# Key products one step ahead in the plain attention steps, and four weight products of layer 3 on a PSUM bank each

## What is computed

```python
def attention(h, ctx, mask, bias, ln_w, w_q, w_k, w_v, w_out):   # layer 1: 32 heads of 128
    q = rmsnorm(h, ln_w) @ w_q.T
    k, v = ctx @ w_k.T, ctx @ w_v.T
    p = softmax(where(mask, q @ k.T + bias, -inf))
    return h + (p @ v) @ w_out.T

def lora(h):                       # layer 2: W_base, 4 active experts of rank 8, a router
    alpha = softmax(log(prior[active] + 1e-12) + (h @ router_W.T + router_b)[active])
    return h @ W_base.T + b_base + sum_e(alpha_e * (h @ A_e.T) @ B_e.T) * 2.0

def cross(h, ctx):                 # layer 3: one head, width 512
    Q, K = h @ Wq.T + bq, ctx @ Wk.T + bk
    return softmax(Q @ K.T / sqrt(512)) @ ctx

def quantised(h):                  # layer 4: 6-bit codes unpacked, scale and zero point
    return h @ dequantise(qweight).T + bias

x = x + attention(layernorm(x), ctx, ...)
x = x + lora(layernorm(x))
x = x + cross(layernorm(x), ctx)
x = x + quantised(layernorm(x))
```

## Time and profile before

| | |
|---|---|
| median of 3 runs | 986.61 us (985.14 to 986.87) |
| profiled execution | 985.75 us |
| its span, first to last instruction | 983.9 us |
| mean granted TensorE clock | 0.994 of full |
| PE busy | 954.6 us, 97% of the span |
| DVE, POOL, ACT busy | 61%, 48%, 40% |
| DMA moved | 169.60 MB, 172 GB/s |

### The profile page before, as it was taken

One profiled execution on the slowest core, in us unless ns is written; L12 is line 12 of the kernel. 1 busy time (PEld: TensorE's weight loads), 2 busy tenths in 40 slices (PEclk: granted clock), 3 DMA queues, 4 the chain that ended last, 5 costly groups with the idle time before them and its releaser, 6 DMA issues.

```text
span 983.9 us, 16715 instructions
## 1 busy us (share of the span) xinstructions
PE 954.6 (97%) x5645; PEld 835.4 (85%) x5645; DVE 603.1 (61%) x1123; ACT 395.0 (40%) x1101; POOL 470.3 (48%) x528
## 2 busy tenths in 40 slices
PE   8999999999999999999999999999999997998995
PEld 7888888888898888888888888888888886776774
DVE  5674773656566566666565656565656577274874
ACT  5655443343434343433333333334343432324553
POOL 2450735464545545555555464555554511022577
PEclk9999999999999999999999999999999999899999
DMA  9233536747474656565555656464747442111001
GB/s 335 88 95 125 171 137 210 261 157 276 156 273 161 257 176 238 190 220 190 217 200 209 219 191 241 168 257 162 256 170 261 151 150 87 52 66 33 1 34 54
DMA packets 58185, 169.60 MB, mean 172 GB/s; under 512 B 5767, under 2 KB 7947, under 8 KB 57884
## 3 DMA queue, kind: packets, MB, share of 16 engines
q1 hardware_dynamic: 58140, 169.01, 48.5%
HBM read 158.51 MB, written 10.49 MB: 172 GB/s over the span
## 4 chain that ended last, share of the span: by engine, by line
PE 91%; DVE 4%; issue 2%; ACT 1%; POOL 1%; DMA 1%; SPq 0%; POOLq 0%; ACTq 0%; DVEq 0%
PE ps_q L325 6%; PE ps_q L326 6%; PE ps_q L327 6%; PE ps_v L325 6%; PE ps_v L327 6%; PE ps_v L326 6%; PE ps_o L325 6%; PE ps_o L327 6%; PE ps_o L326 6%; PE ps_t L1775 6%; PE ps_k L325 6%; PE ps_k L327 6%; PE ps_k L326 6%; PE ps_s L1748 6%; PE ps_t L1765 3%
## 5 line engine op out<-in xcount | busy, mean ns | idle before, releaser
L1203 DVE TENSOR_TENSOR acc<-ps_o,acc 128x512 f32<-128x512 f32 x128 | 87.9, 686 | 153.3 <-PE ps_o L327 153.3
L652 ACT ACTIVATE scores<-scores,neg_max 128x128 f32<-128x128 f32 x256 | 99.9, 391 | 196.3 <-DVE neg_max L1284 196.3
L325 PE MATMUL ps_v<-wv_hi,ct_hi 128*128 128x256 f32 x504 | 143.1, 284 | 1.8 <-DVE vv L1157 1.5
L327 PE MATMUL ps_v<-wv_hi,ct_lo 128*128 128x256 f32 x504 | 142.6, 283 | 0.0
L326 PE MATMUL ps_v<-wv_lo,ct_hi 128*128 128x256 f32 x504 | 142.6, 283 | 0.0
L955 POOL TENSOR_TENSOR wq_lo<-raw_q,wq_hi 128x256 fp32r<-128x256 f32 x65 | 48.2, 742 | 158.6 <-ACT wq_hi L519 158.6
L325 PE MATMUL ps_o<-wo_hi,att_hi 128*128 128x512 f32 x256 | 105.5, 412 | 0.9 <-DVE att_lo L1191 0.9
L658 ACT COPY probs_t<-ps_t 128x512 f32<-128x512 f32 x64 | 37.6, 587 | 168.1 <-PE ps_t L1765 168.1
L325 PEld LDWEIGHTS ps_v<-wv_hi,ct_hi 128*128 128x128 f32 x504 | 96.4, 191 | 6.6 <-issue 2.5
L327 PE MATMUL ps_o<-wo_hi,att_lo 128*128 128x512 f32 x256 | 100.4, 392 | 0.0
L326 PE MATMUL ps_o<-wo_lo,att_hi 128*128 128x512 f32 x256 | 100.2, 391 | 0.0
(11 more groups left out here) (335 smaller groups left out, 2396.9 us busy)
## 6 DMA issues: line engine op xcount, KB each, us to landing
ring_hi<-scratch_x_t SPq DMA_DIRECT2D x39, 512.0 KB, 4.0
ring_lo<-scratch_x_t SPq DMA_DIRECT2D x39, 512.0 KB, 5.0
ring_hi<-scratch_c_t SPq DMA_DIRECT2D x39, 512.0 KB, 4.2
ring_lo<-scratch_c_t SPq DMA_DIRECT2D x39, 512.0 KB, 5.3
raw_v<-in_w_v SPq DMA_DIRECT2D x16, 512.0 KB, 5.7
raw_o<-in_w_o SPq DMA_DIRECT2D x16, 512.0 KB, 3.3
raw_q<-in_w_q SPq DMA_DIRECT2D x15, 512.0 KB, 5.9
raw_k<-in_w_k SPq DMA_DIRECT2D x15, 512.0 KB, 5.6
```

The lines of the kernel that those rows point to most:

```text
L325: pe.matmul(dst, hi_l, hi_r, start=first, stop=False)
L327: return pe.matmul(dst, lo_l, hi_r, start=False, stop=last)
L652: e = act.activation(probs[n][:, m, :], scores[n][:, m, :], ACT.Exp, bias=neg_max[:, n, m:m + 1], accum_out=row_sum[:, n, m:m + 1])
L1203: dve.tensor_tensor(acc[:, b, :], ps_o[:], acc[:, b, :], ALU.add).then_inc(o_added, 1)
```

## The change

Two parts. In the **plain steps** every key product from the fourth on is made one step sooner: step 1 gets `k(4)`, steps 2 to 8 make `k(s + 3)`, and the second key product at the end of step 8 is gone. ACT's copies follow. In the **tail** the four `product_m` go to a bank each, without the wait on `mm_out`; the first three, with the transposes and value products of step 62 between them, stand ahead of the column products. ACT rounds all four after `attention_high(62)` and copies the `kb_row` after them. On PE the scores of step 63 and the first half of step 62's output come ahead of `spread_kb` and the low-rank products, and `product_g(0)` ahead of the LoRA rows. DVE copies the value products of steps 62 and 63 out at the ends of steps 60 and 61, and does `attention_rest(62)` ahead of the vector `uw`. No instruction is added or removed on any engine.

```diff
+        m_banks = (ps_q, ps_k, ps_q2, ps_k2)
...
@@ ACT, step_first
-                if s > 1:
-                    k_evac(s + 2, n, s % 2)
+                if s > 0:
+                    k_evac(s + 3, (s + 3) // 2 % 2, (s + 1) % 2)
...
@@ ACT, tail
-            mm_high(0)
-            mm_high(1)
+            pt_evac(STEPS - 2)
+            attention_high(STEPS - 2)
+            for m in range(NC):
+                mm_high(m)
             act.wait_ge(kb_mm, 1)
             act.copy(kb_row[:], ps_v[:]).then_inc(kb_s, 1)
-            pt_evac(STEPS - 2)
-            mm_high(2)
-            attention_high(STEPS - 2)
...
-            mm_high(3)
             exponentials(STEPS - 1, 1)
...
@@ DVE
-                v_evac(s + 1, ((c + 1) // 2) % 2, (c + 1) % 2)
+                if not (last and c == 5):
+                    v_evac(s + 1, ((c + 1) // 2) % 2, (c + 1) % 2)
...
+                if last and c > 3:
+                    v_evac(s + 2, 1, c % 2)
...
-            v_evac(STEPS - 1, 1, 1)
...
+            attention_rest(STEPS - 2)
             dve.wait_ge(vec_mm, 1)
...
             mm_rest(1)
             mm_rest(2)
-            attention_rest(STEPS - 2)
+            mm_rest(3)
...
-            mm_rest(3)
             step_drain(STEPS - 1, 7)
...
@@ PE, plain steps
-                pe.wait_ge(k_out, min(t, 4 * PLAIN - 2))
+                pe.wait_ge(k_out, t)
...
             output(0, 0, 0, (0,))
+            plain_k(4, 4)
             step_transpose(1, 1)
...
-                plain_k(s + 2, (s + 2) % LOOP_STEPS)
+                plain_k(s + 3, (s + 3) % LOOP_STEPS)
...
-            plain_k(s + 2, 2)
+            plain_k(s + 3, 3)
...
             plain_q(s + 3, 3, ps_q2)
-            plain_k(s + 3, 3, ps_k2)
...
@@ PE, tail
-                wait_from(pe, mm_out, m - 1)
...
             product_m(0)
             output(s - 1, 5, None, (1,))
+            product_m(1)
+            step_transpose(s, 6)
+            product_m(2)
+            step_values(s, 6)
...
             pe.matmul(ps_v[:, NC:NC + 1], ones[:], bqk_sum[:], start=True, stop=True).then_inc(vec_mm, 1)
-            product_m(1)
+            product_m(3)
...
+            s = STEPS - 1
+            step_scores(s, 7)
+            output(s - 1, 6, None, (0,))
             spread_kb()
-            step_transpose(s, 6)
-            product_m(2)
-            step_values(s, 6)
...
             last.then_inc(lr_mm, 1)
-            product_m(3)
-            s = STEPS - 1
-            step_scores(s, 7)
-            output(s - 1, 6, None, (0,))
+            product_g(0)
...
-            product_g(0)
             output(s - 1, 6, None, (1,))
```

More of the change, by code:

```diff
@@ L711, in step @@
                     q_evac(s + 2, 1, 0)
-                    k_evac(s + 2, 1, 0)
+                    k_evac(s + 3, 1, 1)
                 if c % 4 == 0 and more:
@@ L726, in step @@
                     q_evac(s + 3, 1, 1, ps_q2)
-                    k_evac(s + 3, 1, 1, ps_k2)
             for s in range(FIRST):
@@ L762, in mm_high @@
                     act.wait_ge(vec_mm, 1)
-                act.copy(mm_hi[:, m, :], (ps_q, ps_k)[m % 2][:]).then_inc(mm_hi_s, 1)
+                act.copy(mm_hi[:, m, :], m_banks[m][:]).then_inc(mm_hi_s, 1)
             exponentials(STEPS - 2, 0)
-            mm_high(0)
-            mm_high(1)
+            pt_evac(STEPS - 2)
+            attention_high(STEPS - 2)
+            for m in range(NC):
+                mm_high(m)
             act.wait_ge(kb_mm, 1)
             act.copy(kb_row[:], ps_v[:]).then_inc(kb_s, 1)
-            pt_evac(STEPS - 2)
-            mm_high(2)
-            attention_high(STEPS - 2)
             act.wait_ge(lr_mm, 1)
             act.activation(logit_bias[:, 0, :], ps_v[:, 148:152], ACT.Ln, bias=prior_eps[:, 0:1]).then_inc(lbias, 1)
-            mm_high(3)
             exponentials(STEPS - 1, 1)
@@ L1449, in mm_rest @@
                 dve.wait_ge(mm_hi_s, m + 1)
-                dve.tensor_tensor(mm_lo[:, m, :], (ps_q, ps_k)[m % 2][:], mm_hi[:, m, :].bitcast(F32),
+                dve.tensor_tensor(mm_lo[:, m, :], m_banks[m][:], mm_hi[:, m, :].bitcast(F32),
                                   ALU.subtract).then_inc(mm_out, 1)
@@ L1997, in product_m @@
                         pe.wait_ge(w1_lo_s, NC + c + 1)
-                    last = three(pe, (ps_q, ps_k)[m % 2][:], wk1_hi[:, c, cols], wk1_lo[:, c, cols], wq1_hi[:, c, :],
+                    last = three(pe, m_banks[m][:], wk1_hi[:, c, cols], wk1_lo[:, c, cols], wq1_hi[:, c, :],
                                  wq1_lo[:, c, :], c == 0, c == NC - 1)
```

## The result

The changed kernel takes 980.46 us, the median of 5 runs (979.03 to 981.24), beside 986.87 us before (985.14 to 989.29, 5 runs). The ratio is 0.9939, with a 95% interval of 0.9925 to 0.9952. So it is faster, by 6.4 us where 10.0 were predicted, and the time lies 0.26 us above the upper end of the range. The profiled execution, the fastest of the five, took 979.03 us against 985.75: a span of 977.2 us at a mean granted clock of 0.995, where before it was 983.9 at 0.994.

A forecast was written before the change was run, and what follows sets the result against it. PE bounds the kernel, busy 97% of the span, so only its waits and low-clock work pay. Part 1 (-1.8) and part 2 (-8.2) sum to -10.0 us: 975.75 profiled, 976.6 for the median, range 974.7 to 980.2.

The forecast's parts named there:

- Part 1: Plain steps: key products one step sooner fill step 1's 1.41 us wait; +0.82 - 2.72 + 0.10 = -1.8 us.
- The step 1 term: Step 1 gets 0.82 us longer for 2.72 us of key product work, its output's second half ending at 55.27.
- the new wait: Step 5: PE waits about 0.45 us for the key weights' rest; costed at nothing, up to 0.45 if DVE is late.
- the copy before step 9: Step 9's first block product waits for ACT's copy of the last query product: 0 to 0.6 us, taken as 0.1.
- Rival (b): Part 1 gives nothing, through late step 5 weights or ACT's longer queue: 1.8 us lost, 978.4; chance 0.10.
- Part 2: Tail: the 4.8 us wait, low-clock work and smaller waits go, new waits of 0.8 and 1.35 us come; sum -8.2 us.
- the earlier copy of the values: Step 61: `v_evac(63)` ahead of `attention_rest(61)` takes about 0.2 us back from a 0.5 us gain, leaving -0.3.
- +0.2 (between 0 and 0.5): Tail: clock falls again on g(0) and the LoRA rows, its 1.7 us mostly absorbed by the 1.35 us wait for DVE.
- Rival (a): Column products alone bring the low clock, so m(3) runs slow: 2.6 us lost, 979.2; chance 0.18.
- The step that failed: After step 62's second output half, g(1) and layers 2 to 4 hang on the same chain and slide, at no cost.
- Rival (d): Wait and thin work before g(0) bring a lasting low clock; slower, 995 if all eight g products run low; chance 0.04.
- three signs of being wrong: Clock below 1.00 under m(3); wait for `wk_lo` over 1 us; wait over 2 us before step 62's second output half.

The follow-up runs named there:

- the mixed products: Changed kernel with the low-rank products mixed chunk by chunk into g(0) and step 63's softmax ahead of the low-rank evacuations: 973.81 us, ratio 0.9875.
- the tail alone: Changed kernel with the earlier key products undone, so only the tail differs from the kernel before: 980.64 us, ratio 0.9923.
- the ends filled: Changed kernel with matmuls of ones only in the waits before the last two code products: 979.7 us, ratio 0.9933.
- key products alone: Kernel before with only the key products made one step sooner, the tail unchanged: 985.1 us, ratio 0.9977.
- gap filled: Kernel before with 21 matmuls of ones in the 4.8 us wait ahead of the column products: 983.89 us, ratio 0.9986.
- the one wait: Changed kernel with eight matmuls of ones in the 1.76 us wait before the `z_stack` product of batch 0: 977.06 us, ratio 0.9911.
- the six: Changed kernel with matmuls of ones in six waits of PE in layers 2 to 4: 976.6 us, ratio 0.991.
- both edits together: Changed kernel with six waits of layers 2 to 4 filled and the low-rank products mixed into g(0): 973.76 us, ratio 0.9876.

## Why the prediction was wrong

**Part 1, right in mechanism, 0.3 us too large.** The step 1 term was +0.82; the output's second half moved from 54.45 to 55.34, less the 0.08 by which this execution started later: 0.81. The wait for `wk_lo` came with 0.26 us. "I cost the new wait at nothing" was the mis-sized term: between step 1 and step 5 the shift grows from 0.81 to 109.20 - 108.16 - 0.08 = 0.96, so 0.15 us of it were not absorbed, most of it in step 5 (0.84 ahead of it, 0.96 behind). The remaining 0.13 of the 1.8 against 1.52 lie within the guessed 0 to 0.6 for the copy before step 9. Rival (b) is excluded: from the scores of step 1 to the first block product it takes 108.0 us in all eight profiles with part 1, and 109.5 to 109.7 in the four without.

**Part 2, right in its terms, with luck in the tenth.** -8.2 was the sum and -8.2 the measurement in the changed kernel's first profile. The wait of 4.8 us is gone, the wait for the attention tile grew from 0.51 to 0.71 us, which is the 0.2 that the earlier copy of the values was to take back, m(3) takes 2.92 us (2.72 expected), `kb_row` costs 0.68 (0.8). The clock fell on g(0), as forecast from the row at 852 us, and cost 1.6 us, which swallowed the whole 1.35 us wait for DVE. But its size was "+0.2 (between 0 and 0.5)" for a fall of 3.4 us, and in four of the six profiles in which the low-rank products run back to back behind the wait for `kb_row`, it lasted 6.8: there the tail takes 56.0 to 56.1 us, and the term is 1.6 us more. Rival (a) is excluded: the clock is 1.00 at 836.

The fall behind the low-rank products came in all six of those profiles, behind 3.0 us of thin passes with a wait of 0.68 us ahead, and in neither of the two with the mixed products. In the old tail it came in two of four. So thin passes by themselves are not shown to bring it. The rule of the Trainium skill ("TensorE: Matmul & The Clock Gate", Part 1 and its closing table), which asks for no long idle gap between bursts of matmuls and by which the low-rank work does no harm, does not hold here: in the 20 us ahead of the fall at 847.2 the longest wait of PE is 0.68 us. The same Part also tells of a kernel whose short idle times between groups of matmuls made the clock swing, which is nearer to what these traces show.

**The step that failed** is "From the output's second half on, everything (g(1) and on, layers 2 to 4) hangs on the same chain as before and slides." The chain is the same, and its waits are; the clock is not. Two falls came where the profile of before had none: 9.05 us of lead became 7.45 under g(6) and 6.22 by the last code product, 2.8 us given back. I had counted the clock's falls only where the change moves work, and taken the full level behind them for granted. The fall under g(6) was in all five profiles of the new tail in which that wait was not filled (the changed kernel twice, the tail alone, the mixed products, the ends filled), and in none of the four of the old tail (the kernel before twice, key products alone, gap filled). With the wait ahead of it filled it was gone, in three of three profiles (the one wait, the six, and both edits together).

The fall under the code product of batch 6, 1.2 us of the 2.8, is not shown to come of the change. It was in three of the five profiles of the new tail without a fill at the end (the changed kernel twice, the tail alone; not in the one wait filled and the mixed products), and in two of the four of the old one (key products alone, gap filled). The profile that the sum was made against happened to have none.

Rival (d) had this mechanism, low clock on the work behind because "it has waits of its own", but as one lasting fall that costs over 10 us, at 0.04. None of the three signs of being wrong came true: all three lie ahead of the place where the saving was lost.

What stays open is why the old tail spared that wait of 1.76 us, which it has as well. No instruction between the first transposes of layer 2 and the fall differs. When in the execution the wait comes could do it, and nothing here tests that. The falls also differ in length between executions of one program, so a kernel's time is spread (977.59 to 983.49 us for the tail alone, the slow end at the lower clock), and two profiles can differ by a fall without any change.

**The balance**, in the profiled executions: part 1 -1.5, the tail -8.2, a slower loop +0.4, the later start +0.1, the two falls +2.8, and two pieces that I have not followed, +0.2 between the output's second half and layer 2 and -0.5 behind the last code product's start. That is -6.7, and 979.03 - 985.75 = -6.72. The +0.4 is not the change's: 643.24 us before, 643.64 after, but 644.50 when the kernel before was run again.

The range was too narrow for the same reason. It took in rivals and small waits, but no spread of the clock in the 110 us behind the change, where each fall of 3.4 us was worth 1.2 to 1.6. Its high end was also added up wrongly: 976.6 with (a), (b) and 0.5 us of small waits is 981.5; 980.2 holds (a) and 1.0 us alone. That the first median lies 0.26 us outside the range and the second (979.34) inside is luck; the step was wrong in either case.

## What to carry to other kernels

Before a saving is carried to the end of a program, count the stretches at the low clock in more than one profile of before, and allow one more or less at the waits behind the change; here the waits that mattered were of 1.76 us beside thin products and of 2.69 us ahead of a code product. A wait of TensorE that another engine's chain decides can be filled with matmuls nobody reads: here eight products into a free bank cost nothing and gave back what the clock had lost under g(6). Where thin products can be mixed into a dense one and so also cover a wait, try it: it was worth more here than the fills (973.81 against 976.6 us).

## What was not expected of the hardware

- The clock fell behind a wait of only 1.76 us in five of five profiles with one order of the work ahead of it, and in none of four with another, the instructions around it being the same.
- The falls had few lengths, and one place showed more than one of them: 3.4 us (847.2) and 6.8 (846.1) in two executions of the changed kernel, 6.8 (835.2) in the kernel before and 10.2 (831.3) in the key products alone, whose tail is the same. In that last one the clock fell while PE stood idle, 2 us ahead of the next product.
- Twenty thin passes with no wait right ahead of them were followed by a fall in two of four profiles of the old tail, and with a wait of 0.68 us right ahead in six of six of the new one.
- Without any change, the start of step 1 moved by 1.5 us (45.76 to 47.24), and the loop between steps 9 and 60 took either 643.2 to 643.7 or 644.5 us. Together that is more than part 1 of the change is worth, so it was read from its own stretch of the trace and not from the end.
